# A mixture-of-experts kernel on one core: the first loads reordered, the first gate products cut in halves, and the first expert's down products put back by two steps

## The reference

```python
g = jnp.einsum('bsd,edf->ebsf', h, Wg)
u = jnp.einsum('bsd,edf->ebsf', h, Wu)
expert_outs = jnp.einsum('ebsf,efd->ebsd', jax.nn.silu(g) * u, Wd)
expert_output = jnp.einsum('be,ebsd->bsd', gating_probs, expert_outs)
shared = jnp.einsum('bsf,fd->bsd', jax.nn.silu(h @ Sg) * (h @ Su), Sd)
return (1.0 - sg) * expert_output + sg * shared
...
x = x + _L0_cond_ref(x, ...)   # F = 512 hidden features, 8 experts + 1 shared
x = x + _L1_cond_ref(x, ...)   # adapter 128 -> 32 -> 128 by language, then layer norm
```

## Time and profile before

| | us |
|---|---|
| median of 3 runs | 297.24 (296.75 to 297.40) |
| the profiled execution: its own time | 297.04 |
| the profiled execution: span from first to last instruction | 295.2 |
| PE busy | 290.1 (98%) |
| DVE busy | 268.8 (91%) |
| ACT busy | 231.1 (78%) |
| POOL busy | 19.3 (7%) |

### The profile page before, as it was taken

The page is one execution under the profiler, slowest core; times in us unless marked ns, Lnnn a source line. Parts: engine busy times, 40 slices in busy tenths (PEclk is TensorE's granted clock), DMA queues, the critical chain, the costliest instruction groups (busy, mean ns, idle before and its releaser), DMA issues.

```text
span 295.2 us, 5086 instructions
## 1 busy us (share of the span) xinstructions
PE 290.1 (98%) x1510; PEld 144.3 (49%) x1510; DVE 268.8 (91%) x585; ACT 231.1 (78%) x517; POOL 19.3 (7%) x32
## 2 busy tenths in 40 slices
PE   8999999999999999999999999999999999999995
PEld 2444444444444444444444444444444444588883
DVE  5999999998989898988989999999999999977795
ACT  6998878788878787877897788887878876667771
POOL 3200201100000000000002010001100011000011
PEclk9999999999999999999999999999999999999999
DMA  6973110244000000000011001010001110000001
GB/s 208 385 307 109 52 65 19 62 120 112 2 2 0 0 2 0 0 2 1 1 22 26 18 9 39 12 25 19 17 3 39 27 18 10 2 36 3 0 2 36
DMA packets 17940, 13.39 MB, mean 45 GB/s; under 512 B 11486, under 2 KB 15994, under 8 KB 17914
## 3 DMA queue, kind: packets, MB, share of 16 engines
q1 hardware_dynamic: 17482, 12.86, 14.4%
q10 hardware_dynamic: 432, 0.21, 0.2%
HBM read 11.23 MB, written 1.05 MB: 42 GB/s over the span
## 4 chain that ended last, share of the span: by engine, by line
PE 94%; DVE 2%; DMA 1%; SPq 1%; issue 1%; ACT 0%; POOL 0%; POOLq 0%; DVEq 0%
PE moe_ps L449 10%; PE moe_ps L446 10%; PE moe_ps L447 10%; PE gate_ps L400 10%; PE up_ps L426 10%; PE up_ps L431 10%; PE up_ps L423 10%; PE gate_ps L403 10%; PE gate_ps L408 10%; DMA w_full<-weights 1%; DVE hidden L680 1%; PE adapt_ps L458 0%; DVE gx_lo L649 0%; SPq L319 0%; DVE h_lo L686 0%
## 5 line engine op out<-in xcount | busy, mean ns | idle before, releaser
L563 ACT ACTIVATE silu<-gate_ps 128x512 f32<-128x512 f32 (+1 forms) x160 | 88.2, 551 | 45.3 <-PE gate_ps L408 44.3
L680 DVE SCALAR_TENSOR_TENSOR hidden<-silu,up_ps 128x512 f32<-128x512 f32 (+1 forms) x160 | 100.3, 627 | 19.2 <-PE up_ps L431 11.6
L686 DVE TENSOR_TENSOR h_lo<-hidden,h_hi 128x512 f16<-128x512 f32 (+1 forms) x160 | 102.4, 640 | 0.2
L568 ACT ACTIVATE h_hi<-hidden 128x512 f16<-128x512 f32 (+1 forms) x160 | 92.8, 580 | 9.2 <-DVE hidden L680 8.4
L426 PE MATMUL up_ps<-gx_lo,w_hi 128*128 128x512 f16 (+1 forms) x160 | 57.3, 358 | 0.4 <-DVE gx_lo L649 0.4
L400 PE MATMUL gate_ps<-x_hi,w_hi 128*128 128x512 f16 (+1 forms) x160 | 57.4, 359 | 0.0
L431 PE MATMUL up_ps<-gx_hi,w_lo 128*128 128x512 f16 (+1 forms) x160 | 57.3, 358 | 0.0
L423 PE MATMUL up_ps<-gx_hi,w_hi 128*128 128x512 f16 (+1 forms) x160 | 57.3, 358 | 0.0
L403 PE MATMUL gate_ps<-x_lo,w_hi 128*128 128x512 f16 (+1 forms) x160 | 57.3, 358 | 0.0
L446 PE MATMUL moe_ps<-h_hi,w_hi 128*128 128x512 f16 (+1 forms) x160 | 57.3, 358 | 0.0
L449 PE MATMUL moe_ps<-h_lo,w_hi 128*128 128x512 f16 (+1 forms) x160 | 57.3, 358 | 0.0
(11 more groups left out here) (88 smaller groups left out, 148.6 us busy)
## 6 DMA issues: line engine op xcount, KB each, us to landing
w_full<-weights SPq DMA_DIRECT2D x8, 768.0 KB, 9.2
affine_sb<-affine SPq DMA_DIRECT2D x16, 128.0 KB, 2.9
x_full<-xT SPq DMA_DIRECT2D x3, 256.0 KB, 8.6
x<-x_blocks SPq DMA_DIRECT2D x48, 16.0 KB, 1.8
out_dram<-result SPq DMA_DIRECT2D x3, 256.0 KB, 2.1
w_full<-weights SPq DMA_DIRECT2D x4, 128.0 KB, 3.0
w_full<-w2b SPq DMA_DIRECT2D x24, 16.0 KB
w_full<-weights SPq DMA_DIRECT2D x1, 256.0 KB, 3.8
```

Of the source, the lines that this page charges most:

```text
L563: nc.scalar.activation(silu_slot(n), gate_ps[n % 2][:, 0:STEPS[n][4]], ACT.Silu, scale=1.0 / W_SCALE).then_inc(silu_ready, 1)
L568: nc.scalar.activation(h_slot(h_hi, n), hidden_slot(n), ACT.Copy).then_inc(h_hi_ready, 1)
L680: nc.vector.scalar_tensor_tensor(out=hidden_slot(n), in0=silu_slot(n), scalar=HIDDEN_RESCALE, in1=up_ps[n % 2][:, 0:STEPS[n][4]], op0=ALU. ...
L686: nc.vector.tensor_tensor(h_slot(h_lo, n), hidden_slot(n), h_slot(h_hi, n), ALU.subtract).then_inc(h_lo_ready, 1)
```

## The change

**Loads.** SP now issues both halves of x tile 0 first, then w1, w2, w3, x tile 1, w4, and only then the 56 KB of gates. ACT issues w0 first and the 16 KB of gates second.

**First gate products.** `gate(0)` and `gate(1)` become `first_gates()`: the six matmuls of 512 columns become twelve of 256, first for the left half of the columns of both steps, then for the right half.

**Lag of the first down products.** `down_at` gives the steps 0 to 7 a lag of 5 steps (step 0 to 7), which for steps 8 and 9 falls back to 4 and 3. So `down(0)` comes in step 5 where it was in step 3, and step 12 does `down(7)`, `down(8)` and `down(9)`. h_hi and h_lo get six slots where they had four, and hidden four where it had three.

**Order on ACT and DVE.** h_hi and h_lo of steps 0 to 4 come later (`HIDDEN_PARTS_AT`): 0 in step 3, 1 and 2 in step 4, 3 and 4 in step 5. From step 6 on all is as before. w4 is rounded in step 3 (ACT) where it was in step 1. DVE makes the first x_lo before w_lo of w0.

```diff
+FIRST_LAG = 5
+H_SLOTS = 6
-HIDDEN_SLOTS = 3
+HIDDEN_SLOTS = 4
...
 def down_at(n):
-    return n + LAG + min(max(n - len(WHOLE) - len(HALVES) // 2, 0), END_LAG - LAG)
+    first = max(FIRST_LAG - LAG - max(n - 2 * CHUNKS + 1, 0), 0)
+    return n + LAG + first + min(max(n - len(WHOLE) - len(HALVES) // 2, 0), END_LAG - LAG)
...
+HIDDEN_PARTS_AT = {n + 1: [n] for n in range(5, LAST)}
+HIDDEN_PARTS_AT.update({3: [0], 4: [1, 2], 5: [3, 4]})
...
-            load_first(0)
-            sp.dma_start(cols(x_full, 0, HALF), xT[0, :, 0:HALF]).then_inc(x0_loaded[0], 16)
+            for half in range(2):
+                sp.dma_start(cols(x_full, half, HALF), xT[0, :, half * HALF:(half + 1) * HALF]).then_inc(x0_loaded[half], 16)
             for i in (1, 2, 3):
                 load_first(i)
-                if i == 1:
-                    sp.dma_start(gates_in[:, 2 * B:], gates[:, 2 * B:]).then_inc(gates_loaded, 16)
             sp.dma_start(cols(x_full, 1, N), xT[1]).then_inc(x_loaded[0], 16)
             load_first(4)
+            sp.dma_start(gates_in[:, 2 * B:], gates[:, 2 * B:]).then_inc(gates_loaded, 16)
...
+            def first_gates():
+                pe.wait_ge(w_first_hi_ready, 1)
+                for half in range(2):
+                    x_at = slice(half * HALF, (half + 1) * HALF)
+                    pe.wait_ge(x_hi_ready, half + 1)
+                    for n in range(2):
+                        nc.tensor.matmul(gate_ps[n][:, x_at], expert_w(w_hi, 0, 0, n), x_hi[:, x_at], start=True, stop=False)
+                    pe.wait_ge(x_lo_ready, half + 1)
...
-            gate(0)
-            gate(1)
+            first_gates()
...
+            low, high = FIRST_W[0]
+            act.dma_start(w_full[:, low:high], weights[0, :, low:high]).then_inc(w0_loaded[0], 16)
+            nc.scalar.preload_act_table(ACT.Silu)
             act.dma_start(gates_in[:, 0:2 * B], gates[:, 0:2 * B]).then_inc(first_gates_loaded, 16)
-            nc.scalar.preload_act_table(ACT.Silu)
-            act.dma_start(cols(x_full, 1, HALF), xT[0, :, HALF:]).then_inc(x0_loaded[1], 16)
...
+            first_weight_hi(1)
             act.wait_ge(first_coef_ready, 1)
             for q in range(BATCHES):
                 gated_x_hi(0, q)
-            first_weight_hi(1)
...
-                if n > 2:
-                    dve.wait_ge(h_lo_ready, n - 2)
+                if n >= HIDDEN_SLOTS:
+                    dve.wait_ge(h_lo_ready, n + 1 - HIDDEN_SLOTS)
...
-                if n < 2:
-                    first_weight_lo(3 + n)
+                if n == 0:
+                    first_weight_lo(3)
                 if n == 2:
                     for q in range(BATCHES):
                         gated_x_lo(1, q)
-                if n > 0:
-                    hidden_lo(n - 1)
+                if n == 3:
+                    first_weight_lo(4)
+                for m in HIDDEN_PARTS_AT.get(n, ()):
+                    hidden_lo(m)
```

More of the change, by code:

```diff
@@ L62, in down_at @@
 def down_at(n):
-    return n + LAG + min(max(n - len(WHOLE) - len(HALVES) // 2, 0), END_LAG - LAG)
-DOWN_OF = {down_at(n): n for n in range(LAST + 1)}
+    first = max(FIRST_LAG - LAG - max(n - 2 * CHUNKS + 1, 0), 0)
+    return n + LAG + first + min(max(n - len(WHOLE) - len(HALVES) // 2, 0), END_LAG - LAG)
+DOWN_OF = {}
+for n in range(LAST + 1):
+    DOWN_OF.setdefault(down_at(n), []).append(n)
 def last_step(t, at):
@@ L164, in build @@
         hidden = sb("hidden", [P, HIDDEN_SLOTS * N], F32)
-        h_hi = sb("h_hi", [P, CHUNKS * N], F16)
-        h_lo = sb("h_lo", [P, CHUNKS * N], F16)
+        h_hi = sb("h_hi", [P, H_SLOTS * N], F16)
+        h_lo = sb("h_lo", [P, H_SLOTS * N], F16)
         ident = sb("ident", [P, P], F32)
@@ L299, in h_slot @@
             width = STEPS[n][4]
-            low = n % (CHUNKS * N // width) * width
+            low = n % (H_SLOTS * N // width) * width
             return tensor[:, low:low + width]
@@ L394, in gate @@
                     pe.wait_ge(w_hi_ready, 2)
[L395 to L399, removed]
+                pe.wait_ge(silu_ready, n - 1)
                 nc.tensor.matmul(psum, hi, x_hi[:, x_at], start=True, stop=False)
-                if n == 0:
-                    pe.wait_ge(x_lo_ready, 2)
                 nc.tensor.matmul(psum, hi, x_lo[:, x_at], start=False, stop=False)
@@ L405, in gate @@
                     pe.wait_ge(w_lo_ready, lo_count(e, 0))
-                if n in (0, CHUNKS // 2):
-                    pe.wait_ge(w_lo_ready, 1 if n == 0 else 3)
+                if n == CHUNKS // 2:
+                    pe.wait_ge(w_lo_ready, 3)
                 nc.tensor.matmul(psum, lo, x_hi[:, x_at], start=False, stop=True).then_inc(gate_done, 1)
+            def first_gates():
[6 more added lines that the diff above has]
+                    pe.wait_ge(x_lo_ready, half + 1)
+                    for n in range(2):
+                        nc.tensor.matmul(gate_ps[n][:, x_at], expert_w(w_hi, 0, 0, n), x_lo[:, x_at], start=False, stop=False)
+                    pe.wait_ge(w_lo_ready, 1)
+                    for n in range(2):
+                        last = nc.tensor.matmul(gate_ps[n][:, x_at], expert_w(w_lo, 0, 0, n), x_hi[:, x_at], start=False,
+                                                stop=True)
+                        if half == 1:
+                            last.then_inc(gate_done, 1)
             def up(n):
@@ L497, in _ @@
                 up(n)
-                if n in DOWN_OF:
-                    down(DOWN_OF[n])
+                for m in DOWN_OF.get(n, ()):
+                    down(m)
                 for j, (_, _, _, at) in enumerate(JOBS):
@@ L505, in _ @@
             for n in range(LAST + 1, LAST + 1 + END_LAG):
-                down(DOWN_OF[n])
+                down(*DOWN_OF[n])
             _, first, count = TAIL
@@ L605, in _ @@
                 gated_x_hi(0, q)
-            first_weight_hi(1)
             for n in range(LAST + 1):
-                if n == 0:
-                    first_weight_hi(2)
                 silu_of(n)
                 if n < 2:
[L612 to L615, removed]
-                if n > 0:
[L617 to L620, removed]
+                    first_weight_hi(2 + n)
+                if n in (1, 2):
+                    for q in (0, 1):
+                        gated_x_hi(1, 2 * (n - 1) + q)
+                if n == 3:
+                    first_weight_hi(4)
                     act.wait_ge(coef_ready, 1)
+                for m in HIDDEN_PARTS_AT.get(n, ()):
+                    hidden_hi(m)
                 for g, q in GX_AT.get(n, ()):
@@ L777, in _ @@
                                     ALU.mult).then_inc(w_first_hi_ready, 1)
+            first_x_lo(0)
             first_weight_lo(0)
-            first_x_lo(0)
             first_x_lo(1)
```

## The result

| | before | changed |
|---|---|---|
| median of 9 runs | 297.62 us (296.75 to 298.54) | 299.28 us (298.93 to 300.30) |
| ratio | | 1.0058 (95% interval 1.0043 to 1.0074) |
| the profiled execution: time, span | 297.04, 295.2 | 299.55, 297.8 |

The changed kernel is slower by 0.58%, 1.7 us by the medians. The two profiled executions lie 2.51 us apart: the one of before was 0.58 under its median, the one of the changed kernel 0.27 over its own.

The account below looks back on a forecast made before the run. PE, 98% busy, would meet DVE's full list at up(8): X = 7.33 + 12.12 + 0.82 + 0.11 + 0.04 = 20.42, so 1.29 - (20.21 - 20.42) = +1.50 us, median 297.24 to 298.7; forecast +1.0 to +1.9, full range 297.8 to 299.6.

Parts of the forecast that it names:

- The bound: At the third matmul of up(8), PE meets DVE's full list, which must be done through w_lo(1, up) first.
- The down products put back: Six matmuls fewer before the third of up(8), 1.29 us, come back in step 12; change = 1.29 - (20.21 - X).
- X: Start of the third matmul of up(8) in the changed kernel: forecast 20.42, before 20.21, a draw at 18.92.
- hidden(0) starts at 7.33: Start of DVE's full stretch, after silu(0) on ACT and w_lo of w2; 7.31 before, so not moved forward.
- w_lo of w1 now comes behind them at once: On DVE, w_lo of w1 follows gx_lo, which end at 6.2, and is done at 6.6; up(0)'s third matmul stays at 6.65.
- The long first matmuls: First gate products on PE: twelve matmuls of 256 columns at 0.11 take 1.32 us against 1.30 before, costing nothing.
- POOL against DVE: POOL's operations hold DVE's: w_lo of w3 by coef 0.25, gx_lo by x_lo 0.57; 0.82 us lost instead of 0.38.
- late gates: Rival: 56 KB of gates land at 8.6, gate(4) waits until 11.2, two gx_lo held; +1.9 to +2.6 us, chance 0.17.
- the prediction's own rule: A DVE operation on two SBUF tensors starting during POOL's ends as if started 0.13 us before POOL's end.
- Waits between ACT and DVE: hidden(4) on DVE waits for the h_lo(0) just before it: 0.11 us.
- a sign of being wrong: Prediction wrong if DVE pauses, its 25 instructions take under 12 us, hidden(0) starts well before 7.3, or up(8) ends before 19.3.
- First gate at 4.6, the halves nothing, nothing behind step 12: First gate matmul stays at 4.6, half matmuls cost nothing, no later pauses: PE's step 1.94 us, DVE's 1.76.

Follow-up runs that it names:

- e2: Kernel before with only the lag of 5 steps, later h_hi and h_lo, w4 rounded in step 3 and the changed ACT order: 1.0032, 298.62 us.
- e6: Kernel of e2 with h_hi and h_lo spread, one per step from step 3 on, caught up by step 11: 0.9989, 297.49 us.
- e1: Kernel before run again with no edit, as a measure of noise: 0.9993, 297.50 us.
- e5: Changed kernel without the lag: new loads, halves and first ACT and DVE order, but down products, h_hi and h_lo as before: 1.0025, 298.44 us.
- e4: Kernel before with only the new order of load issues on SP and ACT: 1.0008, 297.81 us.
- e8: Changed kernel with the 56 KB of gates issued early, behind w1: 1.0065, 299.67 us.
- e3: Kernel before with only the twelve half-width first gate matmuls: 0.9992, 297.58 us.
- e7: Changed kernel with h_hi and h_lo spread as in e6: 1.0007, 297.81 us.

## Why the prediction was right, and where its sum was off

- **The bound: right.** PE meets DVE's full list at `up(8)`, named with its matmul. e2 and e6 differ in where h_hi and h_lo stand in ACT's and DVE's queues and in slots, and lie 1.3 us apart; the pause is where it was said to be.
- **The down products put back, 1.29 owed: right**, by the table above.
- **The size by medians, +1.50 forecast, +1.66 measured: right, partly by luck.** The sum was made against an execution that was fast for its kernel (X 20.21; e1 has 20.59, and the median before is 0.58 above it). The changed kernel's own X was forecast at 20.42 and was 21.42 in the profiled execution, so between the two traces it was +2.51, outside +1.0 to +1.9. In the medians two errors nearly cancel: the start point too low by 0.58, and the changed kernel slower than the sum by 0.74 (297.04 + 1.50 against 299.28).
- **"hidden(0) starts at 7.33": wrong by 0.84,** the largest mis-sized term. The sum had silu(0) on ACT at 6.0. In the trace ACT was busy with w_hi of w1 and the four gx_hi from 4.93 to 6.51, because their inputs came late: the first gates landed at 4.1 rather than the forecast 3.8, POOL's first operation on them took 0.49 (0.20 in the kernel before), coef was ready only at 4.98, and w1 landed at 4.9 (4.3 in the kernel before). Then silu(0) waited 0.39 more for gate(0). The step "w_lo of w1 now comes behind them at once" also left out that ACT now waits for w1 ahead of gx_hi; in this execution that moved gx_hi by 0.27 at most and silu(0) by nothing, in e5 it is what held hidden(0).
- **The long first matmuls (2.2 us for twelve, forecast 1.3) were not foreseen.** They are the last 0.39 of the 0.84: gate(0) was done only at about 6.85, and silu(0), w_hi and w_lo of w2 and hidden(0) follow in a chain. The other 0.45 is the late inputs; this split is an estimate from the one trace. The long matmuls don't come from the change (e1 and e4 have them), but in the kernel before ACT rounds w2 ahead of silu(0) and stood for w2 until 6.24, behind which they are hidden. The changed kernel has silu(0) first, which lays it open to them.
- **POOL against DVE, 0.82 forecast, 0.68 measured: right in kind.** gx_lo was held as said, coef held nothing. The rival "late gates" had the landing right (9.1, forecast 8.6) but not the price: e8 shows that early gates bring the same clash elsewhere. By the prediction's own rule the first of its two terms (w_lo of w3 held by coef) is 0.20, not 0.25. Whether the 448 B rows of the gates played a part no run here shows. The Trainium skill ("SBUF — State Buffer", "SBUF: two separate sides") says that of a DVE operation with two SBUF inputs and a GpSimd operation that reads SBUF the one that starts first keeps the shared ports for its whole instruction. e8 agrees: w_lo of w3 started during POOL's x_lo and ended at 10.16, 0.28 after it.
- **Waits between ACT and DVE: 0.11 forecast;** hidden(4) came 0.17 late, and the second of the two hidden at 9.10 came 0.21 late, since up(2) ended late. With these, 8.17 + 12.12 + 0.68 + 0.38 + 0.04 = 21.39 of the measured 21.42. DVE stood still for 0.22 us of that, which the prediction had named as a sign of being wrong; it is small beside the 12.97 busy.
- **"First gate at 4.6, the halves nothing, nothing behind step 12": right** (4.58; e3; behind `up(8)` no pause that the kernel before does not have). The figure given for it, 1.76 us of DVE a step, is 2 x 0.60 with 0.30 and 0.26, not 3 x 0.60.

## What to carry to other kernels

Where PE is full and another engine is nearly full beside it, taking PE's work out of a stretch gains nothing unless the other engine's list ahead of the next hand-over gets shorter too: here 1.29 us of matmuls were put back, and DVE's list stayed the same, so they were paid as a pause. Find the instruction at which the two lists meet, and compare what each must do before it; putting h_lo back together with the down products (e6) turned +0.32% into -0.11%. An operation whose operand comes by a late load can hold up others behind it that are ready, as w1 held gx_hi in e5; in the changed kernel itself no run shows a cost of it.

## What the runs showed of the hardware that I had not expected

- **TensorE changes its level at different moments in executions of one program.** The matmuls on zeros ran 0.42 to 0.43 apart for 512 columns, the 1.2 GHz level, and the later ones 0.216, the 2.4 GHz level. The change came at about 4.9 us in the execution shown before, 5.6 in e1, 4.5 in e3, 6.4 in the changed kernel and 7 in e7, after the same eight matmuls without a break. The granted clock reads 1.00 throughout, so only the pitch of the matmuls shows it. The twelve half matmuls of the changed kernel took 0.9 us more than at the high level. Which part of the run-to-run spread (296.6 to 298.6 us for the kernel before) this makes was not measured by itself; in e1 it was none.
- **Moving a small transfer out of the way helped one load and not another.** With the 56 KB of gates behind w4, w2 (3.2 us after its issue at 2.15) landed at 5.3 rather than 6.2, but w1, issued at the same 1.68, at 4.9 rather than 4.3, and gates took 5.0 us where they took 3.7. The gates' place is not what delays w1: with them early again (e8) it landed at 5.2. The landings also differ between executions: the 256 KB of w4 took 3.8 us in the execution shown before, 4.2 in e1 and 5.1 in e3, with the same order of loads.
